# An attention and mixture-of-experts kernel: token rows laid four to a partition, columns put in order when the transposes are evicted

## The reference

```
xn  = layernorm(x)                                   # no weights
out = x + attn(xn) + ffn(xn)

attn(xn): c_q = xn @ W_dq; Q = c_q @ W_uq            # 16 heads of 16
          c_kv = xn @ W_dkv; K = c_kv @ W_uk; V = c_kv @ W_uv
          causal softmax attention, then @ W_o
ffn(xn):  h = layernorm(xn)*ln1_w + ln1_b; causal attention with q, k, v, o weights and biases
          hidden = xn + attention
          xt = layernorm(hidden)*ln2_w + ln2_b
          logits = xt @ router_w                     # 16 experts, the best two of each token
          each token takes a slot (cumulative count in token order) of its two experts, if one of 512 is left
          expert: gelu(xin @ fc1_w + fc1_b) @ fc2_w + fc2_b, times 0.8
          ffn = hidden + weighted sum of the two experts
```

## Time and profile before

| | us |
|---|---|
| median of three runs | 2424.3 |
| lowest, highest | 2418.44, 2435.3 |
| the profiled execution, its own time | 2424.48 |
| its span, first to last instruction | 2422.8 |
| mean granted TensorE clock, share of full speed | 0.947 |

### The profile page before, as it was taken

One profiled execution on the slowest core, in us unless ns is written; L12 is line 12 of the kernel. 1 busy time (PEld: TensorE's weight loads), 2 busy tenths in 40 slices (PEclk: granted clock), 3 DMA queues, 4 the chain that ended last, 5 costly groups with the idle time before them and its releaser, 6 DMA issues. The chain is left out here.

```text
span 2422.8 us, 45249 instructions
## 1 busy us (share of the span) xinstructions
PE 2236.6 (92%) x15977; PEld 1286.5 (53%) x15977; DVE 1901.1 (78%) x5771; ACT 1514.4 (63%) x3190; POOL 507.1 (21%) x405
## 2 busy tenths in 40 slices
PE   5995999999999999999999999999996778999994
PEld 2553444444444444444444444444435667999993
DVE  3553999989899899899899899989917886666661
ACT  2541378778788787787787778878871113545441
POOL 0001000110210201101101001001005115778773
PEclk9997699999999899999899999989997798999997
DMA  5997325345154253451632534516018435666563
GB/s 153 294 264 220 36 28 64 43 57 63 20 73 55 37 64 41 59 63 23 78 44 39 71 38 56 63 21 81 3 19 237 155 86 136 145 137 128 133 130 87
DMA packets 145315, 214.54 MB, mean 89 GB/s; under 512 B 54560, under 2 KB 108000, under 8 KB 136672
## 3 DMA queue, kind: packets, MB, share of 16 engines
q1 hardware_dynamic: 132832, 195.27, 40.8%
q0 software_dynamic: 12288, 16.79, 5.6%
HBM read 138.43 MB, written 76.02 MB: 89 GB/s over the span
## 5 line engine op out<-in xcount | busy, mean ns | idle before, releaser
L653 ACT ACTIVATE probs<-s_banks 128x512 f32<-128x512 f32 (+3 forms) x2560 | 1183.5, 539 | 321.9 <-PE s_banks L604 193.1
L690 DVE TENSOR_REDUCE rowmax<-m_banks 128x1 f32<-128x512 f32 x1536 | 966.5, 683 | 64.8 <-PE m_banks L615 59.2
L615 PE MATMUL m_banks<-ks,qs 48*128 48x512 f32 (+3 forms) x2560 | 827.6, 436 | 28.8 <-PEq L89 20.5
L604 PE MATMUL s_banks<-qs,ks 50*128 50x512 f32 (+3 forms) x2560 | 820.3, 429 | 14.7 <-ACT probs L653 7.7
L633 PE MATMUL v_bank<-probs,vs 128*32 128x512 f32 (+3 forms) x5120 | 616.7, 554 | 0.0
L604 PEld LDWEIGHTS s_banks<-qs,ks 50*128 50x128 f32 x2560 | 402.7, 188 | 394.9 <-ACT probs L653 358.5
L615 PEld LDWEIGHTS m_banks<-ks,qs 48*128 48x128 f32 x2560 | 415.9, 193 | 262.0 <-DVE rowmax L690 163.2
L687 DVE CUSTOM_DVE_ANT_0 unused<-m_banks,c_maskq 128x128 bf16<-128x128 f32 (+3 forms) x1024 | 466.8, 486 | 58.5 <-issue 51.2
L550 POOL CAST nparts<-negmax 128x16 fp32r<-128x16 f32 x64 | 12.6, 196 | 1185.5 <-DVE negmax L696 1185.5
L1432 PE MATMUL e_banks<-w_parts,hid_parts 128*128 128x256 f32 x1536 | 189.7, 284 | 1.4 <-DVE hid_parts L1351 1.4
L576 PE MATMUL s_banks<-c_identb,c_later_col 64*128 64x64 bf16 x1024 | 189.2, 197 | 0.0
(11 more groups left out here) (185 smaller groups left out, 1740.9 us busy)
## 6 DMA issues: line engine op xcount, KB each, us to landing
w<-in_L_ffn_fc_w SPq DMA_DIRECT2D x32, 1024.0 KB, 5.3
qs<-q_scratch SPq DMA_DIRECT2D x96, 256.0 KB, 8.3
ks<-k_scratch SPq DMA_DIRECT2D x96, 256.0 KB, 10.0
q_scratch<-parts SPq DMA_DIRECT2D x64, 256.0 KB, 4.5
k_scratch<-parts SPq DMA_DIRECT2D x64, 256.0 KB, 4.7
v_scratch<-vt SPq DMA_DIRECT2D x16, 512.0 KB, 7.9
v_in<-v_scratch SPq DMA_DIRECT2D x32, 256.0 KB, 10.7
qs<-mrows SPq DMA_DIRECT2D x512, 2.0 KB
```

The costliest lines, as they stand in the source:

```text
L604: ins = pe.matmul(bank, ks[rows, slot, h // 2, k * P:(k + 1) * P], qs[rows, slot, h // 2, q * CH + first:(q + 1) * CH], start=True, stop=n ...
L615: pe.matmul(room(("M", NM * group + n))[:, 0:width], qs[rows, slot, h // 2, t * P:(t + 1) * P], ks[rows, slot, h // 2, c * CH:c * CH + wid ...
L653: act.activation(probs[:, n % PR, 0:width], s_banks[:, (NS * group + n) % SRING, 0:width], ACT.Exp, scale=SCALE).then_inc(p_ready, 1)
L690: dve.tensor_reduce(out, scores, AX.X, ALU.max).then_inc(m_used, 1)
```

## The change

In stages A, C and D the views of x, `xn_dram`, `xt_dram` and `sum_dram` by chunk become `(c p j) d -> c p j d`. Partition p then holds the four neighbouring tokens 4p to 4p + 3 of the chunk, and each transfer moves one piece of 4 KB for each partition where it moved four of 1 KB. The tile j of a chunk is then every fourth token.

Features on the partition stay in token order. For that the evictions of the transposes (units 0 to 3 in stage A, `xtT` in stage C) read the bank as before, tile after tile, and write with a step of four elements, 16 bytes, between neighbours (`by_turns`); and where `attT` meets rows of the new kind, the 128 columns of the stationary operand are taken with that same step. Queries, keys, values, logits and slots are as they were. The number of instructions and of DMAs stays the same.

```diff
+def by_turns(row):
+    return row.rearrange("r (p j) -> r j p", j=TPC)
...
-        x_chunks = x.rearrange("b (c j p) d -> (b c) p j d", j=TPC, p=P)
-        xn_chunks = xn_dram.rearrange("(c j p) d -> c p j d", j=TPC, p=P)
+        x_chunks = x.rearrange("b (c p j) d -> (b c) p j d", j=TPC, p=P)
+        xn_chunks = xn_dram.rearrange("(c p j) d -> c p j d", j=TPC, p=P)
...
+                    if k < 4:
+                        src = src.rearrange("r (j p) -> r j p", j=TPC)
                     if k < 2:
-                        out = xnT[:, k, :]
+                        out = by_turns(xnT[:, k, :])
                     elif k < 4:
-                        out = hT[:, k - 2, :]
+                        out = by_turns(hT[:, k - 2, :])
...
-        xt_chunks = xt_dram.rearrange("(c j p) d -> c p j d", j=TPC, p=P)
+        xt_chunks = xt_dram.rearrange("(c p j) d -> c p j d", j=TPC, p=P)
...
-                        out = xtT[:, k, :]
+                        out, src = by_turns(xtT[:, k, :]), src.rearrange("r (j p) -> r j p", j=TPC)
...
-                            last = pe.matmul(bank[:, j * D:(j + 1) * D], attT[:, c % PLACES, h, tile * P:(tile + 1) * P],
+                            last = pe.matmul(bank[:, j * D:(j + 1) * D], by_turns(attT[:, c % PLACES, h, :])[:, tile, :],
...
-                        pe.matmul(out, attT[:, c % PLACES, h, tile * P:(tile + 1) * P], const["Wo"][:, h, :],
+                        pe.matmul(out, by_turns(attT[:, c % PLACES, h, :])[:, tile, :], const["Wo"][:, h, :],
...
-            tiles = sum_dram[0:T, :].rearrange("(t p) d -> p t d", p=P)
+            tiles = sum_dram[0:T, :].rearrange("(c p j) d -> p c j d", p=P, j=TPC)
...
-                cut = slice(c * TPC, (c + 1) * TPC)
-                sp.dma_start(tiles[:, cut], base[:, cut, :]).then_inc(base_stored, 16)
+                sp.dma_start(tiles[:, c], base[:, c * TPC:(c + 1) * TPC, :]).then_inc(base_stored, 16)
```

## The result

The changed kernel takes 2449.9 us in the median (2442.0 to 2469.2, ten runs), the kernel before 2430.4 (2418.4 to 2445.0, ten runs). The ratio is 1.0085, 95% interval 1.0058 to 1.0111: slower by 19.4 us, where 8.6 were forecast (2433, range 2420 to 2441). The profiled execution of the changed kernel, 2469.2 us, is the slowest of its ten, and that of before, 2424.5, one of its fastest. So totals of the two profiles mislead, and stages have to be compared.

A forecast was written before the change was run, and what follows sets the result against it. TensorE with its evictions bounds stage A, then transfers its tail; VectorE, TensorE close behind, sets C's pace; B is unchanged. Pieces -1.1, A's evictions +8.2, C's +1.5 give +8.6 on 2424.5: 2433 us, range 2420 to 2441.

The forecast's parts named there:

- Stage A, evictions: Stage A: stepped writes add 0.38 us an eviction, 1.52 a chunk, uncovered; first load of the tail 8.2 us later.
- VectorE's reduction: VectorE's maximum over rowmax, reading runs 16 bytes apart: 12 ns over for 16 lone values, priced at 0.74 ns each.
- The rival that the write is free: Evictions in A and C: a stepped write costs nothing, only transfers count, 2423 us; chance 0.32.
- that of four cycles: Evictions in A and C: a lone value costs four cycles, 1.28 us more an eviction, 2465 us in all; chance 0.07.
- Stage A, clock: Stage A: TensorE taken at full clock from 54 to 163 us; only the evictions' 1.52 us a chunk was priced.
- the tail passes the delay on whole and hides chunks 6 and 7: End of stage A: transfer-bound, so the 8.2 us delay carries through and the last two chunks' evictions (3.0 us) are hidden.
- Stage C: Stage C: stepped xtT evictions cost 1.5 us, about 0.5 in each of three low-clock chunks; 3.8 more as upper bound.
- TensorE's slack of 0.78: Stage C, warm chunks: TensorE's 0.78 us wait for xt_now barely covers two evictions' extra 0.76 us.
- the forecast's own sign of being wrong: Stage C changing by more than 4 us would show the forecast wrong, through VectorE and GpSimd meeting at other times.
- Weight loads: Stages C and D: strided stationary loads, at twice the price, 0.21 to 0.23 us, hide under the matmul; cost 0.
- The rival's arithmetic: Stages C and D: loads at three times (0.33 us) show 0.11 each, about 8 us and 5, 2446 in all; chance 0.07.
- Pieces: Stages A and C: 4 KB pieces save 0.12 us per 512 KB on nine path transfers, -1.1 us, bounds 0 and -5.4.

The follow-up runs named there:

- e4: The changed kernel's 16-byte steps on evictions and stationary operand, with pieces kept at 1 KB as in the kernel before: ratio 1.0113 to the kernel before.
- e14: The kernel before with the four evictions of stage A written with a step of eight elements (32 bytes): stage A 244.4 us, no whole time given.
- e9: The changed kernel with twelve more transposes a chunk in TensorE's wait in stage A: 2443.2 us against 2436.4 for the kernel before, ratio 1.0059.
- e7: The kernel before with only the two xnT evictions of stage A written with a 16-byte step: stage A 239.3 us, no whole time given.
- e5: The changed kernel with evictions reading PSUM with the step and writing plain: 2432.8 us against 2429.6 for the kernel before, ratio 1.0003.
- e1: The kernel before with only stage A as in the changed kernel, C and D as before: 2469.0 us against 2432.2, ratio 1.0143.

## Why the prediction was wrong

**Stage A, evictions: right.** 0.38 us each was forecast and is 1.61 / 4 = 0.40, inside the bound of 0.43. Chunks 1 to 5 pay 5 x 1.61 = 8.05 and chunk 0 pays 0.63 (its wait went from 0.87 to 1.50), 8.7 in all for 8.2. The row that it came from, VectorE's reduction, gave 0.74 ns a value; on the path it is 0.79. The rival that the write is free is dead (e4, e14), and so is that of four cycles.

**Stage A, clock: the step that failed.** The forecast put a longer wait of TensorE at the wait's own length. The clock of the work behind it is lowered too, by 1.5 us a time, in three or four chunks of the five. The profile of before showed the clock at 1.00 from 54 to 163 us, with a standstill of 1.20 in each chunk, and I took that level as given. Up to chunk 5, the last before the loads, the changed kernel's L316 starts at 154.85 where it was 142.19, 12.66 later: 8.7 of evictions, less 0.6 for the first load (`x` reached VectorE at 21.14 instead of 21.76), and what is left, 4.6, is the three slow L316. SP's first load followed at 175.54, 12.65 later, and the barrier 12.2. That the tail passes the delay on whole and hides chunks 6 and 7 was right. The price varies with the drops: 12.2 between the first profiles, 16 between the second. Over all profiles A is 242.1 with four dear evictions of 16 bytes (four profiles, e9's filled one apart) and 226.9 with plain ones or 8 bytes (nine), +15.2, where the forecast had 8.2 less the pieces.

The Trainium skill has this on its page TensorE: Matmul & The Clock Gate, section HAM oscillation: a kernel whose TensorE waits long enough between bursts of matmuls starts each burst at the lower clock, and pays the transition every time. e7 is such a kernel: behind a wait of 1.99 us in 23.88 the clock was low in every chunk from the second on, behind 1.54 in 23.04 (e9) in none of those, and behind 2.81 in three or four of five.

**Stage C: mis-sized, by the same step.** Forecast 1.5, upper bound 5.3. Profiles with a plain C and 1 KB pieces have 96.5, 103.8, 99.2, 96.5, 103.3, 99.0 and 98.8, mean 99.6; those with the whole change 103.6, 103.7 and 104.4, mean 103.9: +4.3, inside the bound (with the 107.1 of e9, whose C is the same, 104.7 and +5.1). What failed is, first, that TensorE's slack of 0.78 would cover the two evictions; that wait is on the loop of transposes, `xtT`, logits and the next projections, and TensorE's wait for `xtT` rose by 0.93 a chunk in full. Second, the clock again: one projection more of the last four at the lower clock, 1.5 us. Third, 0.38 a chunk for the loads, put at 0. The 7.1 of the first two profiles is this and scatter. It also set off the forecast's own sign of being wrong, a change of C by more than 4 us; the reason given with that sign, VectorE and GpSimd meeting at other times, did happen (L887, L883), but the intervals above add up without it.

**Weight loads: nearly hidden, at another price.** Twice a plain load was assumed; 324 to 330 ns is nearer to three times the 114 of the earlier trace rows, where the rival began. Still, the loads show as 0.06 us for four in D, not 4 x 0.11, and as 0.38 for 16 in C, not 1.8; D is 94.2 to 95.4 in every kernel. The rival's arithmetic, load minus matmul, was wrong: with a load of 0.33 four times 0.11 did not come on top of the matmuls' own spacing.

**Pieces: right in sign, and worth nothing.** Forecast 0.12 us for 512 KB with bounds 0 and 0.6; the lone loads say 0.21. The first x, forecast to come 0.1 to 0.6 earlier, reaches VectorE at 21.1 to 21.4 us in six of the seven profiles with 4 KB in A and at 21.5 to 21.8 with 1 KB (e9, 21.96, is the exception). In the stage it does not show: plain A with 4 KB 226.8 (three profiles), with 1 KB 227.0 (five). The share of the DMA engines in the early part of A fell from 0.95 to 0.93 at the same pace (e5), where no engine waited for them.

**Sum.** 15.2 + 4.3 = 19.5 of the 19.4 between the medians: the forecast's 8.6, 7.4 more in A and 3.5 more in C. That it meets to 0.1 us is luck: it puts B at nothing, which is 1602 us in the mean of the five profiles with four dear evictions and no filler, and 1595 in the mean of the others, a difference that its scatter of 30 us leaves open. The measured time fell outside the range because the range had a bound for each price and none for what a longer wait does to the work behind it.

**The two pages.** Of the cited rules, SBUF Cachelines of Advanced Engine Details and Errata (the Trainium skill) fits a write too: with two values in their 16 bytes (step of 8) an eviction takes 635 ns, with one alone (step of 16) 1110. The reading of SBUF — State Buffer, section Door 1 (also the Trainium skill), that float32 may be strided four elements for free, does not hold for ScalarE's writes here: two are nearly free, four are not.

**Left open.** Why B takes 1586 to 1616 us with the same instructions; its mean clock was 0.94 in the longest two and 0.96 in the shortest, but no run here sets it. Why e1's runs outdid its stages. What sets off a clock drop: in A the same wait of 2.81 us had one behind it or not. And what puts plain C into its faster or slower pattern.

## What to carry to other kernels

When an eviction has to reorder, put the step on the side that reads PSUM, and write to SBUF without a step: the same permutation took 594 ns that way and 1110 the other. A write with a step of two float32 was nearly free too (635). When a change lengthens a standstill of TensorE, price the work behind it at the lower clock as well; halving the added wait need not halve the loss (e7), and idle repeats on TensorE inside the wait can be cheaper than waiting (e9). Larger pieces are worth a test only where something waits for the transfer.

## What was not expected of the hardware

Two dear evictions cost nearly as much as four: 239.3 us against 240.7, since a clock drop stood in every chunk instead of three in five. Twelve superfluous transposes in a wait made stage A 6 us shorter. ScalarE reads PSUM with a step of 512 bytes at no cost, and at steps of 16 and 32 bytes its writes take 1.9 times as long. In stage C, too, three of the last four projections met the lower clock, at 1.5 us each, where with plain evictions two did.
